# Attention and gated FFN layer on one core: first layernorm in halves, work moved between queues and slots

## The reference

```python
# x: (4, 512, 512) f32; 32 query heads, 8 key/value heads of 16; causal; F = 1376
x = x + attention(layernorm(x))        # q, k with rope; softmax(q k^T / 4) v; @ Wo
x = x + ffn(layernorm(x))              # silu(xt @ Wg^T) * (xt @ Wu^T) @ Wd^T
```

## Time and profile before

| | us |
|---|---|
| median of 3 runs | 824.01 |
| fastest run | 822.51 |
| the profiled execution, time | 827.75 |
| the profiled execution, span from first to last instruction | 826.0 |
| TensorE busy | 778.1 (94%) |
| VectorE busy | 437.5 (53%) |
| ScalarE busy | 345.0 (42%) |
| GpSimd busy | 208.0 (25%) |

### The profile page before, as it was taken

The page is one execution under the profiler, slowest core; times in us unless marked ns, Lnnn a source line. Parts: engine busy times, 40 slices in busy tenths (PEclk is TensorE's granted clock), DMA queues, the critical chain, the costliest instruction groups (busy, mean ns, idle before and its releaser), DMA issues.

```text
span 826.0 us, 12351 instructions
## 1 busy us (share of the span) xinstructions
PE 778.1 (94%) x4449; PEld 529.0 (64%) x4480; DVE 437.5 (53%) x744; ACT 345.0 (42%) x684; POOL 208.0 (25%) x380
## 2 busy tenths in 40 slices
PE   3879999999999999999797999999999999999998
PEld 2645555555555554444385887888878888788886
DVE  6786878677876777887243543423314233241112
ACT  3326667766776677656542332211112111121111
POOL 3134774467526763233300000000000000000000
PEclk9959999999999999999998999999999999999999
DMA  7235677233232335471195110422003210020001
GB/s 254 72 102 175 218 247 230 80 97 111 74 112 73 108 97 185 130 206 36 41 291 151 51 39 13 141 64 66 25 14 130 73 55 34 13 102 0 1 1 51
DMA packets 74614, 81.86 MB, mean 99 GB/s; under 512 B 8721, under 2 KB 58385, under 8 KB 74353
## 3 DMA queue, kind: packets, MB, share of 16 engines
q1 hardware_dynamic: 74560, 81.16, 31.7%
HBM read 57.02 MB, written 33.36 MB: 109 GB/s over the span
## 4 chain that ended last, share of the span: by engine, by line
PE 46%; SPq 2%; DMA 1%; DVE 1%; issue 0%; ACT 0%; DVEq 0%
PE bank L1458 31%; PE ps_y L1510 14%; SPq L1277 1%; SPq L1274 1%; PE bank L1497 1%; DMA inverse<-scratch_inverse 0%; DMA wd_lo<-scratch_wd_raw 0%; DVE x_in L1440 0%; SPq L172 0%; SPq L173 0%; DVE x_res L1444 0%; DVE o_in L185 0%; DVE ctx_lo L195 0%; DVE wd_lo L1384 0%; ACT wd_hi L1332 0%
## 5 line engine op out<-in xcount | busy, mean ns | idle before, releaser
L846 DVE TENSOR_REDUCE m_raw<-ps_s 128x1 f32<-128x512 f32 (+3 forms) x352 | 210.8, 634 | 63.1 <-PE ps_s L1091 60.9
L716 ACT ACTIVATE probs<-ps_t 128x512 f32<-128x512 f32 (+1 forms) x352 | 185.8, 564 | 101.8 <-PE ps_t L1118 100.5
L1415 DVE TENSOR_TENSOR h<-h,bank 128x512 f32<-128x512 f32 (+1 forms) x44 | 30.2, 687 | 221.2 <-PE bank L1458 220.3
L1088 PE MATMUL ps_s<-k_rows,q_rows 96*128 96x256 bf16 (+3 forms) x512 | 132.6, 312 | 6.8 <-DVE m_raw L846 6.1
L1118 PE MATMUL ps_t<-q_rows,k_rows 98*128 98x512 bf16 (+1 forms) x352 | 126.3, 363 | 3.1 <-ACT probs L716 0.9
L1353 ACT ACTIVATE h<-bank 128x512 f32<-128x512 f32 (+1 forms) x44 | 26.3, 599 | 153.4 <-PE bank L1458 153.4
L1088 PEld LDWEIGHTS ps_s<-k_rows,q_rows 96*128 96x128 bf16 x512 | 44.4, 100 | 70.4 <-DVE m_raw L846 32.4
L1131 PE MATMUL ps_o<-probs,v_ones 128*32 128x512 f32 (+3 forms) x1024 | 84.3, 447 | 0.6 <-ACT o_sb L726 0.4
L624 POOL TENSOR_SCALAR_AFFINE_SELECT probs<-probs 128x512 f32<-128x512 f32 x128 | 84.6, 661 | 0.0
L1359 ACT CAST h_hi<-h 128x512 fp32r<-128x512 f32 (+1 forms) x44 | 27.4, 622 | 126.9 <-DVE h L1415 126.9
L217 POOL TENSOR_TENSOR var_eps<-mean_var,eps 128x1 f32<-128x1 f32 x16 | 3.0, 189 | 294.1 <-DVE mean_var L212 294.1
(11 more groups left out here) (146 smaller groups left out, 1349.3 us busy)
## 6 DMA issues: line engine op xcount, KB each, us to landing
scratch_o<-o_sb SPq DMA_DIRECT2D x31, 256.0 KB, 2.4
q_rows<-scratch_q_parts SPq DMA_DIRECT2D x32, 192.0 KB
x_in<-in_x SPq DMA_DIRECT2D x16, 256.0 KB, 4.9
scratch_q_parts<-r_top SPq DMA_DIRECT2D x32, 128.0 KB, 2.4
q_rows<-scratch_q_parts SPq DMA_DIRECT2D x32, 128.0 KB
x_res<-in_x SPq DMA_DIRECT2D x16, 256.0 KB, 2.8
o_in<-scratch_o SPq DMA_DIRECT2D x64, 64.0 KB
inverse<-scratch_inverse SPq DMA_DIRECT2D x64, 64.0 KB
```

The costliest lines, as they stand in the source:

```text
L716: nc.scalar.activation(probs[:, g % 2, heads * u:heads * (u + 1), CHUNK_AT[c]:CHUNK_AT[c + 1]], ps_t[:, pos % S_BANKS, 0:heads * CHUNK_N[c ...
L846: nc.vector.tensor_reduce(out=m_raw[:, g % 2, at:at + heads], op=ALU.max, axis=AXIS.X, in_=ps_s[:, (BANK_AT[i] + u) % S_BANKS, 0:heads * w ...
L1088: nc.tensor.matmul(bank[:, place], q_rows[r][0:ROWS, j, P * q:P * (q + 1)], k_rows[r][0:ROWS, 0:width], start=(place == 0), stop=False)
L1415: nc.vector.tensor_tensor(h[0:m, r], h[0:m, r], bank[units["up", f] % BANKS][0:m, :], ALU.mult).then_inc(h_ready, 1)
```

## The change

It has these parts:

1. Prologue, batch 0: the statistics' mean, the reciprocal root and the normalisation are done for tiles 0, 1 and then for tiles 2, 3. TensorE transposes tile by tile, all four chunks of each, into four banks. ScalarE evacuates the transposes ahead of the query weights' high parts. The key projection waits chunk by chunk. VectorE takes the weight splits after the normalisation.
2. Prologue, batch 1: its statistics and means come after the weight splits and ahead of the keys' rotation, and GpSimd starts the second pair's rotation after batch 1 is normalised.
3. Prologue, DMAs: the key rows of three groups are loaded before their query rows; row 2's store is issued by ScalarE's queue. The low parts of rows 3 and 4 are put later among the row maxima.
4. Last pass: `load_o` two slots earlier; statistics, mean and normalisation each one slot later; units T at gaps 33, 35, 37, 39; the FFN splits after the other work of their slot.
5. Phase 2: the first two tiles of o for batch 1, with their residuals, are loaded between slices 2 and 4 of the weights, not after slice 10.

```diff
-LAST_UNITS = [("W", 0, 10), ("W", 1, 15), ("W", 2, 20), ("W", 3, 25), ("T", 0, 33), ("T", 1, 34), ("T", 2, 35),
-              ("T", 3, 36)]
+LAST_UNITS = [("W", 0, 10), ("W", 1, 15), ("W", 2, 20), ("W", 3, 25), ("T", 0, 33), ("T", 1, 35), ("T", 2, 37),
+              ("T", 3, 39)]
-LAST_XT = {26: 0, 27: 1, 28: 2, 29: 3}
+LAST_XT = {26: 0, 28: 1, 29: 2, 30: 3}
-WO_HI, WO_LO, O_LOAD, CTX_SCALE, CTX_HI, CTX_LO = 2, 4, 2, 5, 6, 7
+WO_HI, WO_LO, O_LOAD, CTX_SCALE, CTX_HI, CTX_LO = 2, 4, 0, 5, 6, 7
-MEAN_AFTER, NORMAL_AFTER = 1, 2
+STATS_AFTER, MEAN_AFTER, NORMAL_AFTER = 1, 2, 3
...
@@ SyncE, prologue
-            for k in range(3):
-                store_rotated(0, k)
+            store_rotated(sp, 0, 0)
+            store_rotated(sp, 0, 1)
             for g in range(3):
-                stage_rows(0, g, g)
-            store_rotated(0, 3)
-            store_rotated(0, 4)
+                stage_rows(0, g, g, "k")
+            for g in range(3):
+                stage_rows(0, g, g, "q")
+            store_rotated(sp, 0, 3)
+            store_rotated(sp, 0, 4)
             stage_max(0)
@@ GpSimd, prologue
-            layernorm_scale(0)
+            layernorm_scale(0, slice(0, 2))
             pool.wait_ge(rstd_ready, 1)
+            layernorm_scale(0, slice(2, 4))
+            pool.wait_ge(rstd_ready, 2)
...
             layernorm_scale(1)
+            pool.wait_ge(xn_ready, TT * 2)
             for s in range(KEY_STEPS + PAIR_STEPS, KEY_STEPS + 2 * PAIR_STEPS):
@@ ScalarE, prologue
+            for kc in range(KC):
+                xt_high(kc, kc)
             act.wait_ge(w_loaded["wq"], DMA)
             for c in range(KC):
                 nc.scalar.copy(w_hi[:, c, 0:D], w_raw[:, c, 0:D]).then_inc(w_hi_ready, 1)
-            for kc in range(KC):
-                xt_high(kc, kc)
...
             rotated_top(0, 2)
+            store_rotated(act, 0, 2)
             raw_rows(0, 4, KC + 4)
@@ VectorE, last pass
-                for after, step in ((0, first_residual), (0, first_statistics), (MEAN_AFTER, first_mean),
+                for after, step in ((0, first_residual), (STATS_AFTER, first_statistics), (MEAN_AFTER, first_mean),
@@ VectorE, prologue
-            for t in range(TT):
-                layernorm_stats(0, t)
-            layernorm_mean(0)
-            split_w(1, w_lo[:, :, D:D + KVW], w_raw[:, :, D:D + KVW], w_hi[:, :, D:D + KVW])
+            for tiles in ((0, 1), (2, 3)):
+                for t in tiles:
+                    layernorm_stats(0, t)
+                layernorm_mean(0, tiles)
             for t in range(TT):
                 layernorm_apply(0, t)
-            for c in range(KC // 2):
-                split_w(2 + c, w_lo[:, c, 0:D], w_raw[:, c, 0:D], w_hi[:, c, 0:D])
+            split_w(1, w_lo[:, :, D:D + KVW], w_raw[:, :, D:D + KVW], w_hi[:, :, D:D + KVW])
             for kc in range(KC):
                 xt_low(0, kc, kc)
-            for c in range(KC // 2, KC):
+            for c in range(KC):
                 split_w(2 + c, w_lo[:, c, 0:D], w_raw[:, c, 0:D], w_hi[:, c, 0:D])
             split_w(KC + 2, w_lo[:, :, D + KVW:], w_raw[:, :, D + KVW:], w_hi[:, :, D + KVW:])
+            for t in range(TT):
+                layernorm_stats(1, t)
+            layernorm_mean(1)
             dve.wait_ge(tables_loaded, 2 * DMA)
...
-            for t in range(TT):
-                layernorm_stats(1, t)
-            layernorm_mean(1)
             for t in range(TT):
                 layernorm_apply(1, t)
...
-            row_max(0, 0, 0, [lambda: rotated_low(0, 3)])
-            row_max(0, 0, 1, [lambda: rotated_low(0, 4)])
+            row_max(0, 0, 0)
+            row_max(0, 0, 1, [lambda: None, lambda: rotated_low(0, 3)])
...
-            row_max(1, 1, 0, [lambda: max_low(0)])
+            row_max(1, 1, 0, [lambda: max_low(0), lambda: None, lambda: rotated_low(0, 4)])
@@ TensorE, project and prologue
-                if kind == "R" and k == 0 and c == 0:
-                    pe.wait_ge(dense_evacuated, unit)
+                if kind == "R" and k == 0 and (c == 0 or unit == KC):
+                    pe.wait_ge(dense_evacuated, c + 1 if unit == KC else unit)
...
+            for t in range(TT):
+                pe.wait_ge(xn_ready, t + 1)
+                for kc in range(KC):
+                    mm = nc.tensor.transpose(dense_bank(kc)[:, P * t:P * (t + 1)], xn[:, t, P * kc:P * (kc + 1)], ident[:])
+                    if t == TT - 1:
+                        mm.then_inc(dense_ready, 1)
@@ SyncE, phase 2
                 if has_next:
-                    if not positive(b):
-                        sp.wait_ge(inverse_stored, DMA)
-                    for t in range(2):
+                    for t in range(2) if positive(b) else ():
                         load_next_o(b + 1, t)
                         load_next_residual(b + 1, t)
...
-            for f in range(1, FIRST + 1):
-                load_ffn(f)
+            load_ffn(1)
+            load_ffn(2)
+            load_next_o(1, 0)
+            load_next_residual(1, 0)
             sp.wait_ge(recip_done, 1)
             sp.dma_start(row_inverses(d, B - 1), sums).then_inc(inverse_stored, DMA)
+            load_ffn(3)
+            load_next_o(1, 1)
+            sp.wait_ge(inverse_stored, DMA)
+            load_next_residual(1, 1)
             for f in range(FIRST + 1, FT):
                 load_ffn(f)
```

More of the change, by code:

```diff
@@ L368, in top_bits, with store_rotated @@
             return tile.bitcast(BF16).rearrange("p (t two) -> p t two", two=2)[:, :, 1]
+        def store_rotated(queue, b, k):
+            queue.wait_ge(r_top_ready, N_ROPE * b + k + 1)
+            queue.wait_ge(r_lo_ready, N_ROPE * b + k + 1)
+            for part in range(PARTS):
+                tile = r_low[:, k % 2] if part == PARTS - 1 else r_top[:, k % 2, part]
+                for half in range(2) if k == 0 else ():
+                    queue.dma_start(d["k_parts"][b, :, part, HALF * half:HALF * (half + 1)],
+                                 tile[P // 2 * half:P // 2 * (half + 1)]).then_inc(r_stored[0], DMA)
+                if k:
+                    pair, half = (k - 1) // 2, (k - 1) % 2
+                    queue.dma_start(d["q_parts"][b, PAIR_HEADS * pair:PAIR_HEADS * (pair + 1), part,
+                                              HALF * half:HALF * (half + 1)], tile).then_inc(r_stored[k], DMA)
         block = ctx.enter_context(nc.Block())
@@ L392, in copy_raw, with stage_rows @@
                 sp.dma_start(d[name + "_raw"][at], d[name][at]).then_inc(raw_copied, DMA)
[L394 to L410 removed]
+            def stage_rows(b, g, n, tiles=("k", "q")):
+                if n >= RING:
+                    sp.wait_ge(scores_t_ready, t_count(n - RING, T_BANKS_OF - 1))
+                if "k" in tiles and g == 0:
                     sp.wait_ge(r_stored[0], R_STORE[0] * (b + 1))
[L412 removed]
+                if "q" in tiles and g % 4 == 0:
                     sp.wait_ge(r_stored[1 + g // 2], R_STORE[1] * (b + 1))
                     sp.wait_ge(r_stored[2 + g // 2], R_STORE[1] * (b + 1))
[L415 to L416 removed]
                 r = n % RING
@@ L422, in stage_rows @@
                     rows = slice(at, at + DH * times)
-                    sp.dma_start(q_rows[r][rows], heads[:, 0:times].rearrange("j p w t -> (p w) j t")
-                                 ).then_inc(rows_staged[r], DMA)
-                    sp.dma_start(k_rows[r][rows], d["k_parts"][b, g, part].unsqueeze(0).broadcast_to([times, DH, T])
-                                 ).then_inc(rows_staged[r], DMA)
+                    if "k" in tiles:
+                        sp.dma_start(k_rows[r][rows], d["k_parts"][b, g, part].unsqueeze(0).broadcast_to(
+                            [times, DH, T])).then_inc(rows_staged[r], DMA)
+                    if "q" in tiles:
+                        sp.dma_start(q_rows[r][rows], heads[:, 0:times].rearrange("j p w t -> (p w) j t")
+                                     ).then_inc(rows_staged[r], DMA)
                     at += DH * times
@@ L485, in iteration @@
                     if has_next and slot - 1 in LO_SLOT:
-                        store_rotated(b + 1, LO_SLOT[slot - 1])
+                        store_rotated(sp, b + 1, LO_SLOT[slot - 1])
                     if i == 0 and n + 3 < GROUPS:
@@ L537, in _, with layernorm_scale @@
             pool.wait_ge(consts_ready, 1)
-            def layernorm_scale(b):
-                pool.wait_ge(ln_mean, TT * (b + 1))
-                nc.gpsimd.tensor_tensor(var_eps[:], mean_var[:, :, 1], eps[:], ALU.add).then_inc(var_ready, 1)
-                pool.wait_ge(var_ready, b + 1)
-                nc.gpsimd.tensor_tensor(rstd[:], var_eps[:], half[:], ALU.pow).then_inc(rstd_ready, 1)
+            def layernorm_scale(b, tiles=slice(0, TT)):
+                n = tiles.start // 2 if b == 0 else b + 1
+                pool.wait_ge(ln_mean, TT * b + tiles.stop)
```

(7 more changed lines are left out.)

28 lines of the change are left out of this document (6 added, 22 removed).

## The result

The changed kernel takes 810.62 us (median of 4 runs, 808.24 to 811.23); the kernel before took 823.26 beside it (4 runs). The ratio is 0.9828, with a 95% interval of 0.9802 to 0.9854: 1.7% faster. In us the medians differ by 11.9 to 12.6. The forecast of 805.0 was 5.6 us too low, its range of 797 to 813 holds the time. The profiled execution took 811.23, its span is 809.5 us, where before it was 826.0. A second profile of the kernel before has a span of 824.6.

A forecast was written before the change was run, and what follows sets the result against it. TensorE was taken as the bound, so gains come only where it stands still. 8.5 - 3.3 + 3.4 + 3.2 + 7.2 = 19.0 us, taken from a median of 824.0, gave 805.0 us, range 797 to 813.

The forecast's parts named there:

- start: Prologue: earlier normalisations, projection, keys and row loads bring the first scores sooner; gain 8.5 us, bounds 6 and 10.5.
- first group of the last pass: Last pass, first group: o's loads delay the maxima's transfer, stopping TensorE and halving its clock; cost 3.3 us, bounds 1.0 and 6.
- tile 3 of o: Last pass: its load no longer follows the FFN weights, so stop and half clock go; gain 3.4 us, bounds 2.5 and 3.8.
- last transposes: End of last pass: spreading transposes removes stops, less 1.2 us for exponentials' copies; gain 3.2 us, bounds 0 and 5.
- phase 2: Batch 1's tile of o loaded earlier removes TensorE's 5.18 us stop and its slow clock; gain 7.2 us, bounds 4 and 7.4.
- with 2.5 us to land, the first scores start at 39.7: Start: the first group's three query loads, issued by 37.1, land 2.5 us later; first scores at 39.7 instead of 47.94.
- Rival D: Last pass, first group: no stop, since the same weights bound the maxima's transfer either way; 802 us, chance 0.17.
- rival A: Last pass: SyncE falls behind, four groups' maxima come late, 27 us against other gains of 23; 828 us, chance 0.03.
- the cover of 1.5 us: Phase 2: context ready at 438, TensorE wants it at 439.4; once this slack is gone, each us costs one.
- C: Phase 2: the o load's delay is only exchanged for slice 4's; gain 4 instead of 7.2, 808.2 us, chance 0.1.
- B: Start held by SyncE and ScalarE ordering (rows or maxima late), and tail gives nothing; gain 12.3, 811.7 us, chance 0.2.
- the 0.66 on more than 2%: Whole kernel: chance 0.66 of being faster by over two per cent (16.5 us, or 807.5); same 0.31, slower 0.03.

The follow-up runs named there:

- second pair: Changed kernel and kernel before, both unedited, run and profiled again: medians 811.04 and 825.03 us, spans 810.0 and 824.6 us.
- O_LOAD = 1: Changed kernel with a tile of o's loads in the last pass right behind the maxima's transfer, not ahead of it: 807.05 us, ratio 0.9784 to the kernel before.
- O_LOAD = 2: Changed kernel with the last pass's loads of o as late as in the kernel before: 810.93 us, ratio 0.9832 to the kernel before.
- second measurement: Changed kernel without edit, measured again beside other runs: 811.04 us, ratio 0.9828, against 825.03 us for the kernel before.

## Why the prediction was right, and where it was short

The mechanisms were right at each of the five places; the sum was 2.5 us too large for the profiled execution (16.5 instead of 19.0) and the step from there to the median cost another 3.1. The table sets the forecast beside both pairs of profiles. Its places are cut at TensorE's transposed scores: the first of all, those of the last pass before group 1, those before and after tile 3, and the border of the phases.

| term | forecast | first pair | second pair |
|---|---|---|---|
| start, to the first transposed scores | 8.5 | 6.5 | 5.4 |
| from there to the last pass | none | -0.4 | -1.1 |
| first group of the last pass | -3.3 | -2.7 | -2.4 |
| tile 3 of o | 3.4 | 3.6 | 1.9 |
| last transposes | 3.2 | 2.2 | 3.6 |
| phase 2 | 7.2 | 7.3 | 7.1 |
| sum | 19.0 | 16.5 | 14.6 |

**Start: the step that failed.** VectorE's steps came within 0.6 us up to the keys (20.10 for 20.6), and the last normalisation was 1.5 us early (32.0 for 33.5), since four cost 1.90 and not 2.77. That price was misread: the 2.77 us of the earlier trace rows was not free of GpSimd, whose memsets ran beside it from 9.98. GpSimd's contention is real, at 0.60 us for two (1.57 against 0.97), but its source was those memsets, not the power: the power ran from 8.11 beside the first two, and they took 0.97. The second normalisations end at 10.60, exactly as forecast, by two errors that cancel. The wrong step is "with 2.5 us to land, the first scores start at 39.7". It gave the three query loads the DMA engines to themselves, but six more are issued right behind them and share the engines; they took until 42.2. Holding the six back gave 39.71. With the loads held the first transposed scores were at 54.51 and 54.90, 8.9 and 8.6 us sooner than the 63.45 on which the term of 8.5 was made, so the landing is what it lacked. Over nine traces it came 0.6 to 2.7 us later than forecast; 42.2 is near the late end. The second normalisation and the transposes, at which I looked for the next latest work, were done at 38.

**Behind the start** the forecast had put nothing. TensorE ran at half clock from the first scores on, to about 58 us in the changed kernel's first profile and 60 in its second, and by the last pass it had lost 0.4 and 1.1 us against the kernel before. That the clock is the whole cause of this isn't shown.

**Maxima's transfer in the last pass.** Issue order decided with O_LOAD = 0: the issue came at 323.88, 5.3 us behind the first load of o, and TensorE waited 2.58 to 3.07 us in all seven traces of kernels with that order. The forecast had 2.3 instead of 0.4, and 1.6 for the clock; these make 3.5, not its 3.3. Against O_LOAD = 1 the cost was 3.0 to 3.3. Rival D (bound by the weights either way, so no loss) is refuted: in the changed kernel the weights had landed at 323.10, before the maxima were issued, and with O_LOAD = 1 the loss was gone. Its mechanism exists, though: with O_LOAD = 2 the wait went with the weights' landing, as far as four traces show, and the cost was 0 to 2.4 us. Against such an execution of the kernel before, the change loses less than 3.3 here. (In rival A the other gains add up to 22.3 by the terms, not to its 23.)

**Tile 3** came as forecast in the first pair, where the stop's half clock counts, and at 1.9 us in the second, where the kernel before had the stop without it. The later slots of statistics, mean and normalisation cost nothing that the trace shows. **Last transposes:** the first stop went with its clock, the exponentials took back 1.08 as forecast (1.2), the fourth transpose waits still (1.22), for which 0.4 had been taken off and 1.2 were due. The second pair has 3.6 us here, so a size of 2.2 is one pair's. **Phase 2:** phase 2 begins 9.15 us sooner, so the forecast's times, which count from the old 411.76, have to be read 9.15 less. Slice 4's first load leaves at 419.80 (forecast 428, so 418.9), its parts have landed at 425.35 (433 to 434, so 424 to 425), and the context is ready at 429.87 (438, so 428.9). TensorE wants it at 430.14 as forecast. Each step was within 1 us and all of them erred to one side: of the cover of 1.5 us only 0.3 is left, and the gain is the whole 7.3 because it held. Rivals A and C did not happen; of B, the rows' half did, at 2.5 us here and 0.6 to 2.7 over the traces, while the tail still gave.

**From the trace to the median.** The forecast subtracted a sum made against one execution from the median of others. The kernel before had its profiled execution 3.7 us above its median, the changed kernel 0.6 above. Of these 3.1 us, 1.4 are seen: the second profile of the kernel before is that much shorter, 0.8 of it in the start. The rest I can't place. With it the gain in the medians is 12.6 us beside the same runs (13.4 against the 824.0 of the table, 14.0 in the second measurement), not 19. So the time is 1.7% lower, and the 0.66 on more than 2% was too much.

**What stays open:** why the megabyte of weights lands after 5.7 to 6.2 us in most executions and after 7.4 and 8.2 in two; how often the kernel before has the long one; whether it is the weights that hold the maxima back; and how much of the query rows' lateness is the six loads behind them, about 1.4 us by the mean of the traces.

## What to carry to other kernels

When a transfer is on the path, count the loads issued right behind it too: in the traces here it was earliest with none behind it. A small, urgent transfer belongs ahead of long ones that aren't due, but ask what waits for the long ones before they are moved. Make a sum against several profiles of the kernel before, if they are to be had: a stop that depends on a landing differs by 1 to 2 us from execution to execution, and a sum made against a long one promises too much.

## What the runs showed of the hardware

- Three row loads of a group fed their reader 4.2 and 4.6 us after the first issue (at 39.7 and 40.1) when nothing followed until they had landed, and after 4.6 to 6.4 us (at 40.3 to 42.4 in nine traces) when six more followed at once.
- Four normalisations of a tile (128x512, float32) take 1.90 us with GpSimd idle, 2.97 beside its multiplications on 128x512 tiles, and before 5.71. With the memsets of 2x512 beside them two took 1.57 instead of 0.97, and four 2.77; one took 0.82 us beside a memset and 0.54 without.
- A DMA issue on ScalarE's queue took as long as on SyncE's: three stores 1.26 and 0.64 us, in which ScalarE did nothing else, against 1.17 and 0.62 when SyncE issued them.
- What the granted clock did behind a stop differed between executions. Behind the stop of 1.80 us at tile 3 it was 0.50 in 374 to 376; behind one of 1.75 at the same place, in the kernel's second profile, it stayed at 1.00. Behind the maxima's stop of 2.93 us the changed kernel's scores took 0.63 us; behind 3.07, in its second profile, matmuls took 0.39 us for 1.0 us more, until 329.5, and then 0.55 to 0.63.
